# Projection, gate, up and down matmuls issued as four 32-column tiles inside a loop of 32-column tiles

## The chip, the cores and the metric

One core of one Trainium2 chip runs the whole kernel. The metric is device time in microseconds (us). The inputs are float32 (the feed-forward weights int32), the output is float32.

## What is computed

One transformer layer with adaptive layer norm over 2048 tokens of width 128 and 16 heads of width 8:

```python
h = _layernorm(x) * (1 + ca) + sa
x = x + ga * attention(h)      # 16 heads, softmax over 2048 keys, out @ Wo.T, clipped and projected
h = _layernorm(x) * (1 + cb) + sb
gate = h @ wg.T; up = h @ wu.T # wg, wu: 384 x 128, dequantised from int32
x = x + gb * ((silu(gate) * up) @ wd.T)
```

## The kernel before

The queries are cut into four blocks (`Bk`) of 512. A block is a loop of 64 steps: four groups of four heads, and for each group 16 tiles of 128 keys. In a step `j`

- `score` (line 686) multiplies 128 keys by 512 queries for four heads. The 128 keys are four **column tiles**: each matmul has 32 weight columns and writes 32 of the 128 output partitions, and `tile_position=(0, 32 * c)` says which quarter of TensorE's array it takes. Four matmuls in four quarters run at the same time. A step has 16 of them, bf16.
- ScalarE takes the exponential of the scores, 128x1024 at a time, twice in a step (line 506).
- `product(j - 1)` (line 702) multiplies the values by the exponentials of the step before. It is four float32 matmuls in four quarters, one for each head; the trace shows a float32 matmul as two weight loads and two matmul records, called passes in what follows, so a product has 8 records.

The closing work of block `Bk - 1` (output projection, residual, layer norm, feed-forward) is done while block `Bk` runs. Its place is written out by hand: TensorE issues its part behind `product` in fixed steps, `AT_WO` = 7 (output projection, line 711), `AT_TR` = 14 (transposes, line 718), `AT_GATE` = 18, 22, 27 (line 725), `AT_UP` = 20, 25, 30 (line 730) and `AT_DOWN` = 36, 38, 40, 42 (line 737). These matmuls have 128 weight columns and take the whole array. Gate and up are one matmul of 512 moving columns each (two passes). The output projection is four matmuls of 128 moving columns (8 passes), and a down step is three of them (6 passes). ScalarE takes a tanh (line 521) behind each gate, and it does so in the order written: in a gate step the tanh stands behind the step's two exponentials.

The last block's closing work has nothing to run beside it. It stands at the end: `t_wo`, seven and two filler matmuls (`keep_warm`, line 660) around the transposes, three gates and three ups in banks of their own, and 12 down matmuls (line 797).

TensorE's queue is in order. `score` of a step waits until ScalarE has emptied one of three PSUM slots, `product` waits for the exponentials of its own step.

Of the kernel before, what the change touches and what calls it, by code (L numbers as in the profile page):

```python
# [30 lines left out]
P = 128  # L31
# [10 lines left out]
CW = 32  # L42
COLS = P // CW
HID = 384
NM = HID // P
# [13 lines left out]
DOWN_BANK = (0, 3, 6, 7)  # L59
# [16 lines left out]
def build(nc, x, columns, wmod, fixed, w1t, w2t, w_att, wgt, wut, wdt, out):  # L76
    with ExitStack() as ctx:
        def sb(name, shape, dt=F32):
            return ctx.enter_context(nc.sbuf_tensor(name, shape, dt))

        def sem(name):
            return ctx.enter_context(nc.semaphore(name))
# [10 lines left out]
        wk_sb, wv_sb, wq_sb, wo_sb = (w_att_sb[:, i, :] for i in range(4))  # L93
# [16 lines left out]
        wg_f, wu_f = sb("wg_f", [P, HID]), sb("wu_f", [P, HID])  # L110
        wd_f = sb("wd_f", [P, NM, D])
# [13 lines left out]
        def tmp(words, *shape, dt=F32):  # L125
            v = arena[:, at[0]:at[0] + words]
            at[0] += words
            assert at[0] <= ARENA
            if dt != F32:
                v = v.bitcast(dt)  # L130
            if len(shape) == 2:
                v = v.rearrange("p (a b) -> p a b", a=shape[0])
            return v
# [32 lines left out]
        att_T = tmp(BT)  # L166
# [5 lines left out]
        h2_T = tmp(BT)  # L172
        th = [tmp(BT) for _ in range(NM)]
        gl = [tmp(BT) for _ in range(NM)]
        hid = tmp(NM * BT, NM, BT)
# [15 lines left out]
        def bank(i):  # L191
            return ps[:, i, :]
# [5 lines left out]
        O_bank, M_bank = bank(6), bank(7)  # L198
# [10 lines left out]
        S = {n: sem(n) for n in names}  # L209
# [332 lines left out]
        def _(pe):  # L542
# [3 lines left out]
            for i in range(2):  # L546
                ins = pe.matmul(bank(6 + i)[:, 0:3 * D], silu_b[:, :], wmod_sb[:, 3 * D * i:3 * D * (i + 1)],
                                start=True, stop=True)
# [108 lines left out]
            def keep_warm(n, to):  # L657

                for _ in range(n):
                    ins = pe.matmul(to, ones_bf[:, 0:P], ones_bf[:, 0:BT], start=True, stop=True)  # L660
                ins.then_inc(S["warm"], 1)
# [32 lines left out]
            def product(Bk, j):  # L694

                g, kt = divmod(j, NT)
                pe.wait_ge(S["exped"], Bk * 2 * STEPS + 2 * j + 2)
                if kt == 0 and not (isinstance(Bk, int) and Bk == 0 and g == 0):
                    pe.wait_ge(S["o_evac"], Bk * NG + g)
                for i in range(GH):  # L700
                    h = GH * g + i
                    ins = pe.matmul(O_bank[32 * i:32 * (i + 1), :], V_op[:, kt, VW * h:VW * h + 32],  # L702
                                    probs[:, 2 * (j % 2) + i // 2, BT * (i % 2):BT * (i % 2 + 1)],
                                    start=kt == 0, stop=kt == NT - 1, tile_position=(0, 32 * i))
                if kt == NT - 1:
                    ins.then_inc(S["pv_done"], 1)

            def t_wo(Bk):
                pe.wait_ge(S["norm"], Bk + 1)
                for t in range(TPB):  # L710
                    ins = pe.matmul(M_bank[:, P * t:P * (t + 1)], att_T[:, P * t:P * (t + 1)], wo_sb,  # L711
                                    start=True, stop=True)
                ins.then_inc(S["wo_ps"], 1)

            def t_transpose(Bk):
                pe.wait_ge(S["h2_done"], Bk + 1)
                for t in range(TPB):
                    ins = pe.transpose(M_bank[:, P * t:P * (t + 1)], h2[:, t, :], ident_sb)  # L718
                ins.then_inc(S["h2T_ps"], 1)

            def t_gate(Bk, m, to):
                pe.wait_ge(S["h2T_done"], Bk + 1)
                if m and to is M_bank:
                    pe.wait_ge(S["glu_done"], Bk * NM + m)
                pe.matmul(to, wg_f[:, P * m:P * (m + 1)], h2_T, start=True, stop=True).then_inc(S["gate_ps"], 1)  # L725

            def t_up(Bk, m, to):
                if to is M_bank:
                    pe.wait_ge(S["gated"], Bk * NM + m + 1)
                pe.matmul(to, wu_f[:, P * m:P * (m + 1)], h2_T, start=True, stop=True).then_inc(S["up_ps"], 1)  # L730

            def t_down(Bk, to, tiles=range(TPB)):
                if tiles[0] == 0:
                    pe.wait_ge(S["glu_done"], Bk * NM + NM)
                for t in tiles:
                    for m in range(NM):
                        ins = pe.matmul(to[:, P * t:P * (t + 1)], hid[:, m, P * t:P * (t + 1)], wd_f[:, m, :],  # L737
                                        start=m == 0, stop=m == NM - 1)
                if tiles[-1] == TPB - 1:
                    ins.then_inc(S["down_ps"], 1)  # L740

            def block_steps(Bk, tails, p):
                for j in range(STEPS):
                    score(Bk, j, p)
                    if j:
                        product(Bk, j - 1)
                    elif tails:
                        product(Bk - 1, STEPS - 1)
                    if tails:
                        if j == AT_WO:  # L750
                            t_wo(Bk - 1)
                        if j == AT_TR:
                            t_transpose(Bk - 1)
                        if j in AT_GATE:
                            t_gate(Bk - 1, AT_GATE.index(j), M_bank)
                        if j in AT_UP:
                            t_up(Bk - 1, AT_UP.index(j), M_bank)
                        if j in AT_DOWN:
                            t_down(Bk - 1, M_bank, [AT_DOWN.index(j)])

            def blocks(p):
                first, last = NB * p, NB * (p + 1) - 1
                if p == 0:
                    pe.wait_ge(S["K_ones"], 16)
                else:
                    pe.wait_ge(S["Q_loaded"], 16 * QUERY_LOADS * first)
                block_steps(first, False, p)
                if p == 0:
                    pe.wait_ge(S["ffn_ready"], 3)
                if p == 0:  # L770
                    for Bk in range(first + 1, last + 1):
                        pe.wait_ge(S["Q_loaded"], 16 * QUERY_LOADS * Bk)
                        block_steps(Bk, True, p)
                else:
                    with pe.Fori(first + 1, last + 1) as Bk:
                        pe.wait_ge(S["Q_loaded"], 16 * QUERY_LOADS * Bk)
                        block_steps(Bk, True, p)
                product(last, STEPS - 1)

                pe.wait_ge(S["o_evac"], NG * (last + 1))  # L780
                pe.matmul(bank(0)[96:128, :], place_num, O_sb[:, NG - 1, :], start=True, stop=True,
                          tile_position=(0, 96))
                pe.matmul(bank(1)[96:128, :], place_den, O_sb[:, NG - 1, :], start=True, stop=True,
                          tile_position=(0, 96)).then_inc(S["placed"], 1)
                t_wo(last)
                pe.wait_ge(S["epow_out"], 2 * (last + 1))
                keep_warm(7, bank(5))
                t_transpose(last)
                keep_warm(2, bank(5))
                for m in range(NM):  # L790
                    t_gate(last, m, bank(m))
                    t_up(last, m, bank(3 + m))

                for m in range(NM):
                    pe.wait_ge(S["glu_done"], last * NM + m + 1)
                    for t in range(TPB):
                        ins = pe.matmul(bank(DOWN_BANK[t])[:, P * t:P * (t + 1)], hid[:, m, P * t:P * (t + 1)], wd_f[:, m, :],
                                        start=m == 0, stop=m == NM - 1)
                ins.then_inc(S["down_ps"], 1)
                if p == 0:  # L800
                    pe.wait_ge(S["flag_in"], 1)
                    pe.matmul(bank(2)[0:1, 0:1], flag_f[:, 0:1], flag_f[:, 1:2], start=True, stop=True)\
                        .then_inc(S["flag_ps"], 1)
# [8 lines left out]
            with pe.If(pe.value_load(flag_i[0:1, 0:1], min_val=0, max_val=1)):  # L812

                q_all = q_slot(0)
                with pe.Fori(0, NB) as b:
                    pe.wait_ge(S["max_loaded"], 16 * PARTS * (b + 1))
                    for h in range(H):
                        for t in range(TPB):
                            pe.wait_ge(S["max_taken"], b * (H * TPB) + h * TPB + t + 1)
                            for i in range(NB):  # L820
                                ins = pe.matmul(bank(i), q_all(h, SHIFT_ROW)[:, P * t:P * (t + 1)],
                                                K_op[0:SHIFT_ROW, h, BT * i:BT * (i + 1)], start=True, stop=True)
                            ins.then_inc(S["max_scores"], 1)
                    pe.wait_ge(S["max_taken"], (b + 1) * (H * TPB) + 1)
                    for t in range(TPB):
                        ins = pe.transpose(M_bank[0:H, P * t:P * (t + 1)], mx[:, t, :], ident_sb)
# [434 lines left out]
```

## Time and profile before

| | us |
|---|---|
| median of 3 runs | 625.63 |
| lowest and highest | 624.21, 626.75 |
| the profiled execution: its time | 624.65 |
| its span, first to last instruction | 622.8 |
| TensorE busy | 565.1 |
| ScalarE busy | 526.5 |

The span is what the rows below divide up; 1.85 us lie outside it. Busy times of TensorE are of overlapping records, whose ends are modelled.

### The profile page before, as it was taken

To read this page: it belongs to the slowest core of one execution; us is meant where nothing else is said; L and a number is where in the kernel's file an instruction comes from. 1 tells how busy PE (TensorE), PEld (TensorE's weight loads), DVE (VectorE), ACT (ScalarE), POOL (GpSimd) and SP (SyncE) were. 2 spreads that over 40 slices of the span, in tenths; PEclk is the share of its full clock that TensorE was granted. 3 is DMA by queue.
4 is the path that set the end of the run, shared out by engine and by line. 5 is a ranking of instruction groups with operands and counts; after the bars stand their busy time and mean duration, and the time that the engine had idled before them with its cause. 6 is when DMAs were issued, how large, how long until landed. Compare 5 with 4: busy or idle time off the path is not lost.

```text
span 622.8 us, 14892 instructions
## 1 busy us (share of the span) xinstructions
PE 565.1 (91%) x6482; PEld 207.4 (33%) x6482; DVE 144.4 (23%) x403; ACT 526.5 (85%) x607; POOL 20.1 (3%) x23
## 2 busy tenths in 40 slices
PE   1688299999999999999999999999999999999635
PEld 0353033333333333333333333343333333433123
DVE  7957400000000531100004510000026110010264
ACT  3575499999999999899999989889999989899501
POOL 2300100000000000000000100000001000000010
PEclk9599599999999999999999999999999999999959
DMA  6014566610000400000004000000000000000000
GB/s 183 2 59 96 119 131 128 113 30 11 3 8 6 82 6 6 1 11 18 11 1 87 2 9 1 11 18 11 1 11 2 10 1 9 2 23 5 2 0 22
DMA packets 15617, 19.50 MB, mean 31 GB/s; under 512 B 2255, under 2 KB 13711, under 8 KB 15263
## 3 DMA queue, kind: packets, MB, share of 16 engines
q1 hardware_dynamic: 14927, 16.96, 12.8%
q0 software_dynamic: 336, 1.18, 0.6%
q8 instruction: 52, 0.85, 0.6%
q10 hardware_dynamic: 288, 0.40, 0.2%
q14 instruction: 14, 0.11, 0.1%
HBM read 12.10 MB, written 4.19 MB: 26 GB/s over the span
## 4 chain that ended last, share of the span: by engine, by line
PE 50%; ACT 33%; issue 8%; DVE 5%; DMA 3%; SPq 1%; POOL 0%; ACTq 0%
ACT probs L506 30%; PE ps L702 19%; PE ps L686 19%; DMA q_scr<-arena 2%; PE ps L725 2%; PE ps L730 2%; PE ps L737 2%; PE ps L660 1%; DVE probs L914 1%; PE ps L711 1%; DMA x_tm<-x_dram 1%; PE ps L597 1%; PE ps L603 1%; SPq L257 1%; PE ps L577 1%
## 5 line engine op out<-in xcount | busy, mean ns | idle before, releaser
L506 ACT ACTIVATE probs<-ps 128x1024 f32<-128x1024 f32 x512 | 473.9, 1084 | 21.4 <-PE ps L686 21.3
L702 PE MATMUL ps<-probs,V_op 128*32 128x512 f32 x2048 | 271.6, 602 | 1.7 <-ACT probs L506 1.1
L686 PE MATMUL ps<-Q_op,K_op 73*32 73x512 bf16 x4096 | 269.4, 379 | 1.0 <-ACT probs L506 1.0
L686 PEld LDWEIGHTS ps<-Q_op,K_op 73*32 73x32 bf16 x4096 | 114.7, 96 | 204.5 <-issue 135.2
L702 PEld LDWEIGHTS ps<-probs,V_op 128*32 128x32 f32 x2048 | 44.8, 108 | 94.2 <-ACT probs L506 85.8
L1055 DVE COPY O_sb<-ps 128x512 f32<-128x512 f32 x16 | 11.1, 691 | 254.5 <-PE ps L702 254.5
L357 POOL TENSOR_TENSOR small<-small,half 128x4 f32<-128x4 f32 x4 | 4.1, 1014 | 504.0 <-DVE small L1108 504.0
L1137 DVE SCALAR_TENSOR_TENSOR arena<-arena,ps 128x512 f32<-128x512 f32 x12 | 8.2, 687 | 43.6 <-ACT arena L521 43.6
L516 ACT ACTIVATE arena<-ps 128x512 f32<-128x512 f32 x4 | 2.4, 597 | 18.6 <-PE ps L718 18.6
L1143 DVE TENSOR_TENSOR arena<-ps,arena 128x512 f32<-128x512 f32 x12 | 8.3, 691 | 42.3 <-PE ps L730 42.2
L554 PE MATMUL ps<-fixed_sb,arena 128*128 128x128 f32 x32 | 6.8, 356 | 12.0 <-POOL arena L363 11.1
L1155 DVE TENSOR_TENSOR arena<-ps,mod 128x512 f32<-128x512 f32 x3 | 2.1, 692 | 63.4 <-PE ps L737 63.4
L660 PE MATMUL ps<-ones_bf 128*128 128x512 bf16 x16 | 7.2, 621 | 7.8 <-POOL small L357 7.8
L1078 DVE RECIPROCAL arena<-arena 128x512 f32<-128x512 f32 x4 | 13.4, 3354 | 0.1
L725 PE MATMUL ps<-arena,wg_f 128*128 128x512 f32 x24 | 13.3, 636 | 0.0
L730 PE MATMUL ps<-arena,wu_f 128*128 128x512 f32 x24 | 13.2, 632 | 0.0
L521 ACT ACTIVATE arena<-ps 128x512 f32<-128x512 f32 x12 | 7.2, 597 | 6.9 <-PE ps L725 6.9
L737 PEld LDWEIGHTS ps<-wd_f,arena 128*128 128x128 f32 x72 | 8.9, 190 | 10.1 <-issue 10.1
L620 PE MATMUL ps<-arena,hs_bf 128*16 128x512 bf16 x4 | 1.7, 434 | 10.9 <-ACT arena L452 10.9
L737 PE MATMUL ps<-wd_f,arena 128*128 128x128 f32 x72 | 11.2, 292 | 0.0
L451 ACT ACTIVATE arena<-arena 128x512 bf16<-128x512 f32 x4 | 2.5, 622 | 10.3 <-DMA q_scr<-arena 8.0
L711 PE MATMUL ps<-w_att_sb,arena 128*128 128x128 f32 x32 | 5.5, 326 | 5.7 <-DVE arena L1082 5.7
(150 smaller groups left out, 251.8 us busy)
## 6 DMA issues: line engine op xcount, KB each, us to landing
K_op<-k_scr SPq DMA_DIRECT2D x36, 128.0 KB
Q_op<-q_scr SPq DMA_DIRECT2D x9, 384.0 KB
arena<-O_sb SPq DMA_DIRECT2D x120, 16.0 KB
k_scr<-probs SPq DMA_DIRECT2D x9, 128.0 KB, 1.8
q_scr<-arena POOLq DMA_DIRECT2D x3, 384.0 KB, 15.0
Q_op<-q_scr SPq DMA_DIRECT2D x12, 96.0 KB
x_tm<-x_dram SPq DMA_DIRECT2D x4, 256.0 KB, 4.6
out_dram<-arena SPq DMA_DIRECT2D x4, 256.0 KB, 2.3
```

The costliest lines, as they stand in the source:

```text
L506: act.activation(probs[:, 2 * (j % 2) + half_, :], slot_bank(u % 3), ACT.Exp)\
L660: ins = pe.matmul(to, ones_bf[:, 0:P], ones_bf[:, 0:BT], start=True, stop=True)
L686: ins = pe.matmul(slot_bank(u % 3)[CW * c:CW * (c + 1), i, :], K_op[0:rows, h, at_k:at_k + CW], Q_op[0:rows, at_q:at_q + BT], start=True, ...
L702: ins = pe.matmul(O_bank[32 * i:32 * (i + 1), :], V_op[:, kt, VW * h:VW * h + 32], probs[:, 2 * (j % 2) + i // 2, BT * (i % 2):BT * (i % 2 ...
L711: ins = pe.matmul(M_bank[:, P * t:P * (t + 1)], att_T[:, P * t:P * (t + 1)], wo_sb, start=True, stop=True)
L725: pe.matmul(to, wg_f[:, P * m:P * (m + 1)], h2_T, start=True, stop=True).then_inc(S["gate_ps"], 1)
L730: pe.matmul(to, wu_f[:, P * m:P * (m + 1)], h2_T, start=True, stop=True).then_inc(S["up_ps"], 1)
L737: ins = pe.matmul(to[:, P * t:P * (t + 1)], hid[:, m, P * t:P * (t + 1)], wd_f[:, m, :], start=m == 0, stop=m == NM - 1)
L1055: dve.tensor_copy(O_sb[:, g, :], O_bank).then_inc(S["o_evac"], 1)
L1078: c.did(dve.reciprocal(rec_T, rec_T))
L1137: dve.scalar_tensor_tensor(gl[m], th[m], 1.0, gates, ALU.add, ALU.mult).then_inc(S["gated"], 1)
L1143: dve.tensor_tensor(hid[:, m, :], ups, gl[m], ALU.mult).then_inc(S["glu_done"], 1)
```

## The change

Each of these matmuls with 128 weight columns becomes four matmuls with 32, written to the four quarters of the same output. The moving operand, the data type, the places in the order and the waits stay as they are. The transposes and the filler matmuls are not touched.

```diff
+            def by_columns(to, weights, moving, start=True, stop=True):
+                for c in range(COLS):
+                    ins = pe.matmul(to[CW * c:CW * (c + 1), :], weights[:, CW * c:CW * (c + 1)], moving,
+                                    start=start, stop=stop, tile_position=(0, CW * c))
+                return ins
+
             def t_wo(Bk):
                 pe.wait_ge(S["norm"], Bk + 1)
                 for t in range(TPB):
-                    ins = pe.matmul(M_bank[:, P * t:P * (t + 1)], att_T[:, P * t:P * (t + 1)], wo_sb,
-                                    start=True, stop=True)
+                    ins = by_columns(M_bank[:, P * t:P * (t + 1)], att_T[:, P * t:P * (t + 1)], wo_sb)
                 ins.then_inc(S["wo_ps"], 1)
...
-                pe.matmul(to, wg_f[:, P * m:P * (m + 1)], h2_T, start=True, stop=True).then_inc(S["gate_ps"], 1)
+                by_columns(to, wg_f[:, P * m:P * (m + 1)], h2_T).then_inc(S["gate_ps"], 1)
...
-                pe.matmul(to, wu_f[:, P * m:P * (m + 1)], h2_T, start=True, stop=True).then_inc(S["up_ps"], 1)
+                by_columns(to, wu_f[:, P * m:P * (m + 1)], h2_T).then_inc(S["up_ps"], 1)
...
-                        ins = pe.matmul(to[:, P * t:P * (t + 1)], hid[:, m, P * t:P * (t + 1)], wd_f[:, m, :],
-                                        start=m == 0, stop=m == NM - 1)
+                        ins = by_columns(to[:, P * t:P * (t + 1)], hid[:, m, P * t:P * (t + 1)], wd_f[:, m, :],
+                                         start=m == 0, stop=m == NM - 1)
...
-                        ins = pe.matmul(bank(DOWN_BANK[t])[:, P * t:P * (t + 1)], hid[:, m, P * t:P * (t + 1)], wd_f[:, m, :],
-                                        start=m == 0, stop=m == NM - 1)
+                        ins = by_columns(bank(DOWN_BANK[t])[:, P * t:P * (t + 1)], hid[:, m, P * t:P * (t + 1)],
+                                         wd_f[:, m, :], start=m == 0, stop=m == NM - 1)
```

## Rows read from the trace of the kernel before

**Rows 1.** Busy time by stretch: first block, second block, the closing work at the end.
```profile
core 0: us, PE busy (x) PEld busy (x) DVE busy (x) ACT busy (x) POOL busy (x), PEclk, DMA share, GB/s
77.80:195.20 117.40, 116.65 (x1529) 40.22 (x1528) 2.74 (x8) 116.94 (x130) 0.00 (x0) 1.00 0.29 56
195.40:324.50 129.10, 128.72 (x1588) 45.85 (x1584) 22.67 (x52) 120.94 (x133) 2.05 (x2) 1.00 0.08 17
...
593.20:622.80 29.60, 14.99 (x59) 8.91 (x59) 15.84 (x50) 2.39 (x4) 2.01 (x2) 0.73 0.04 11
```

**Rows 2.** ScalarE by line in the second block: count, busy and mean, idle before, releaser.
```profile
L506 ACT ACTIVATE probs<-ps 128x1024 f32<-128x1024 f32 x129 | 120.0, 1071 | 7.0 <-PE ps L686 7.0
L521 ACT ACTIVATE arena<-ps 128x512 f32<-128x512 f32 x3 | 1.8, 597 | 1.2 <-PE ps L725 1.2
```

**Rows 3.** Timeline of ScalarE through the down steps: start, us, work, idle before.
```profile
268.73 3.78 ACT L506 ACTIVATE probs<-ps 128x1024 f32<-128x1024 f32 x4
273.26 3.77 ACT L506 ACTIVATE probs<-ps 128x1024 f32<-128x1024 f32 x4 [0.75 <-PE ps L686]
...
286.82 5.61 ACT L506 ACTIVATE probs<-ps 128x1024 f32<-128x1024 f32 x6 [0.75 <-PE ps L686]
```

**Rows 4.** Timeline of TensorE, a plain step.
```profile
207.78 1.06 PE L702 MATMUL ps<-probs,V_op 128*32 128x512 f32 x8
208.67 1.05 PE L686 MATMUL ps<-Q_op,K_op 73*32 73x512 bf16 x16
```

**Rows 5.** Timeline of TensorE around a down step and the step behind it.
```profile
270.73 1.07 PE L702 MATMUL ps<-probs,V_op 128*32 128x512 f32 x8
271.73 0.94 PE L737 MATMUL ps<-wd_f,arena 128*128 128x128 f32 x6
272.59 1.05 PE L686 MATMUL ps<-Q_op,K_op 73*32 73x512 bf16 x16
273.46 1.03 PE L702 MATMUL ps<-probs,V_op 128*32 128x512 f32 x8
274.32 1.04 PE L686 MATMUL ps<-Q_op,K_op 73*32 73x512 bf16 x16
```

**Rows 6.** Timeline around the output projection.
```profile
209.62 1.07 PE L702 MATMUL ps<-probs,V_op 128*32 128x512 f32 x8
210.61 1.16 PE L711 MATMUL ps<-w_att_sb,arena 128*128 128x128 f32 x8
211.70 1.05 PE L686 MATMUL ps<-Q_op,K_op 73*32 73x512 bf16 x16
212.37 1.02 ACT L506 ACTIVATE probs<-ps 128x1024 f32<-128x1024 f32 x1 [0.97 <-PE ps L686]
```

**Rows 7.** Timeline around the first gate (232.46) and the first up (237.17).
```profile
231.46 1.07 PE L702 MATMUL ps<-probs,V_op 128*32 128x512 f32 x8
232.46 1.12 PE L725 MATMUL ps<-arena,wg_f 128*128 128x512 f32 x2
233.52 1.05 PE L686 MATMUL ps<-Q_op,K_op 73*32 73x512 bf16 x16
233.62 0.60 ACT L521 ACTIVATE arena<-ps 128x512 f32<-128x512 f32 x1 [0.41 <-PE ps L725]
234.19 3.77 ACT L506 ACTIVATE probs<-ps 128x1024 f32<-128x1024 f32 x4
...
236.18 1.06 PE L702 MATMUL ps<-probs,V_op 128*32 128x512 f32 x8
...
237.17 1.13 PE L730 MATMUL ps<-arena,wu_f 128*128 128x512 f32 x2
238.23 1.05 PE L686 MATMUL ps<-Q_op,K_op 73*32 73x512 bf16 x16
...
238.90 1.94 ACT L506 ACTIVATE probs<-ps 128x1024 f32<-128x1024 f32 x2 [0.94 <-PE ps L686]
```

**Rows 8.** Gate and product by line: durations in ns, least, median, most.
```profile
L725 PE MATMUL ps<-arena,wg_f x24: 592/593/697, 232.5 to 611.8; 128*128 128x512 f32 x24
...
L702 PE MATMUL ps<-probs,V_op x2048: 589/593/617, 80.9 to 584.2; 128*32 128x512 f32 x187
```

**Rows 9.** Timeline of TensorE in the closing work at the end.
```profile
593.23 2.07 PE L711 MATMUL ps<-w_att_sb,arena 128*128 128x128 f32 x8 [5.74 <-DVE arena L1082]
...
607.84 1.13 PE L725 MATMUL ps<-arena,wg_f 128*128 128x512 f32 x2
608.80 1.02 PE L730 MATMUL ps<-arena,wu_f 128*128 128x512 f32 x2
...
612.24 1.02 PE L730 MATMUL ps<-arena,wu_f 128*128 128x512 f32 x2
613.10 2.84 PE L797 MATMUL ps<-wd_f,arena 128*128 128x128 f32 x24
```

**Rows 10.** Records begun in a tenth of a microsecond, at a product (columns as in the first group).
```profile
229.70:229.80 0.10, 0.06 (x4) 0.09 (x8) 0.00 (x0) 0.10 (x1) 0.00 (x0) 1.00 0.00 0
```

## The prediction

> **What bounds the kernel now.** I read the busy time by stretch first. The first block, which carries no closing work, takes 117.4 us for 64 steps, 1.83 us each, and ScalarE is busy for 116.94 of them; the second block takes 129.1 us, and ScalarE is busy for 120.94 [rows 1]. So the exponentials set the pace of a plain step: two of them at 0.92 us. TensorE has little to spare, though. Scores and product without a wait between them take 0.87 + 0.86 = 1.73 us (273.46 less 272.59, and 274.32 less 273.46) [rows 5], which leaves 0.10 us a step. Anything put into TensorE's order beyond that starves ScalarE.
>
> Next, ScalarE by line in the second block, to see how it waits. It stood idle for 7.0 us before exponentials, always for scores, and for 1.2 us before the three tanh, for the gate matmuls [rows 2]. The timeline says where: 0.97 us behind the output projection [rows 6], 0.94 behind an up, 0.41 before a tanh [rows 7], 0.75 behind each of four down steps [rows 3]. 0.97 + 3 x 0.94 + 4 x 0.75 is 6.8 of the 7.0. These 8 us are what the change can take from a block; the other 3.5 of the 11.7 that block two has over block one are mainly the copy and the tanh themselves, which stay.
>
> **What a closing matmul costs in TensorE's order.** I measure it from the start of the product before it to the start of the scores behind it, less the 0.89 us that this takes in a plain step [rows 4].
> - down: 272.59 - 270.73 - 0.89 = 0.97 us [rows 5]
> - output projection: 211.70 - 209.62 - 0.89 = 1.19 [rows 6]
> - gate: 233.52 - 231.46 - 0.89 = 1.17; up: 238.23 - 236.18 - 0.89 = 1.16 [rows 7]
>
> A gate is two passes of 512 columns. One pass takes 0.43 us: eight of them lie between 608.80 and 612.24 [rows 9]. Two are 0.86, so 0.31 us of the 1.17 are not streaming. Part of it is seen in the durations: the first gate pass has 697 ns where most have 593, 0.10 more, a weight load that nothing hides; a product behind a wait has 617, 0.02 more [rows 8], for a quarter of the columns. The remaining 0.2 is silence on either side, where full-width and quarter-width matmuls meet. Where quarter meets quarter there is none: product to scores takes 0.86 [rows 5], float32 followed by bf16, just two passes.
>
> A short pass, 128 moving columns at full width, takes (2.84 - 0.275)/23 = 0.112 us in the last 24, with 0.275 the duration of one record, worked out from the modelled end [rows 9].
>
> **The change part by part.** In the new form a gate or up is what `product` already is: eight records in four quarters, 0.86 us, with the weights of the next pass loaded under the present one [rows 5]. That takes the gate from 1.17 to 0.86 and the up from 1.16 to 0.86.
>
> A short pass in quarters is not in the trace. From below it can't beat a quarter of a long one, 0.43/4 = 0.107. From above, the densest sustained stream there is is the scores, four pairs of weight load and matmul in 0.87/4 = 0.217 us [rows 5]. I take 0.11: right after an event wait eight loads and four matmuls begin inside 0.10 us [rows 10], so four pairs in 0.11 us ask for little more than TensorE does here, and 32 weight columns expose 0.02 us where 128 expose 0.10 [rows 8], so the loads fit under a pass. The output projection is then 8 x 0.11 = 0.88 instead of 1.19, a down step 6 x 0.11 = 0.66 instead of 0.97. Each of the eleven insertions of a block gets 0.30 to 0.31 us shorter.
>
> **What of it reaches ScalarE.** For the eight without a tanh, idle time is insertion less 0.22: 0.97 for 1.19, 0.94 for 1.16, 0.75 for 0.97. The same 0.22 each time means that TensorE alone sets these waits, and that the next steps don't make them good. The new insertions stay above 0.22, so the whole saving arrives: 0.31 + 3 x 0.30 + 4 x 0.31 = 2.45 us a block.
>
> In a gate step the tanh stands between. It starts when the gate is done, 2.16 us after the product's start (233.62 - 231.46) [rows 7]. New: 0.89 for the product, 0.43 to the second pass, 0.59 for that record, 0.04 for the semaphore, 1.95. The tanh comes 0.21 earlier, and the exponential behind it 0.57 after the tanh, at 1.95 + 0.57 = 2.52. The scores would let it start at 0.89 + 0.86 + 0.67 = 2.42 (0.67 is scores to exponential, 238.90 - 238.23 [rows 7]), so the tanh decides: 3 x 0.21 = 0.63 us a block.
>
> A block saves 2.45 + 0.63 = 3.1 us, three blocks 9.3. The first block has no closing work and stays.
>
> At the end everything is on the path. The output projection runs at the low clock (mean 0.73 in this stretch [rows 1]), its 8 passes are streaming, and only the first load shrinks: 0.1. The first gate pass has 593 + 104 ns there too, gain 0.08; the five projections behind it follow without gaps and stay; 24 down passes gain 24 x 0.002 = 0.05 [rows 9]. Sum 0.2.
>
> All in all 9.5 us. From the profiled execution's 624.65 that is 615.2; the median of the runs lies 1.0 above that execution, so 625.63 - 9.5 = 616.1 us. What the edit costs is instructions: 3 more pairs for each of the old, 528 pairs in all. What hides them is the streaming of the passes themselves, 0.11 us for four pairs; without that cover the third rival below holds.
>
> **A rule and the rows.** Why the 0.2 us of silence vanishes is no row's to tell: no full-width matmul behind quarter-width ones comes without it. The Trainium skill ("TensorEngine Tiling (Array Packing)", Key Properties) says that changing the tiling mode, and not merely the tile, drains TensorE. By that rule the silence goes with the change, and the sum is the 9.5 us. Were it a matter of the closing work itself, only the weight load would shrink, and the sum would be the second rival's.
>
> **Rivals.**
> 1. *The sum holds* (0.68): 616.1, with its own range 614.8 to 618. The lower end is passes of 0.107 (0.3 us) and the scatter of a median of few runs, the upper one gates and ups that give 0.2.
> 2. *The silence stays*: only the weight loads shrink, 0.10 to 0.02, 0.08 us x 33 insertions + 0.2 = 2.8 us, 622.8. Against it: quarter after quarter has no silence at any of the places shown. 0.07.
> 3. *The short passes are bound by issue*, the case on the other side. Four pairs must be issued where one was, and a short pass gives them 0.11 us. There are 32 short passes in each of three blocks and 24 at full clock at the end, 120. The gain of 9.5 is used up when a pass takes 0.11 + 9.5/120 = 0.19 us; above that the kernel is slower. At 0.217, the pace of the scores, it is 120 x 0.107 = 12.8 lost, 3.3 net: 628.9. At the pace of a whole step, 24 pairs in 1.73, a pass takes 0.29, and it is 638. For it: nothing in the trace issues faster for longer than a dozen instructions. Against it: those dozen, at 0.008 us each [rows 10]. 0.10. The Trainium skill ("TensorE: Matmul & The Clock Gate", the section on the gap of 56 ns) has two floors that bear on it, about 25 ns from matmul to matmul, which four in 0.11 us just meet, and about 62 ns a matmul where ucode decodes, which would make a pass 0.25. This trace's four matmuls inside 0.1 us speak against the second.
> 4. *The short passes are a little long*: four loads of 0.02 to 0.03 us one behind the other instead of together make a pass some 0.135. 120 x 0.025 = 3 us given back: 619.1, range 618 to 621.5. 0.12.
>
> The remaining 0.03 is for what I don't see, half of it a wait that the earlier output projection meets.
>
> **How the numbers follow.** A measurement of this kernel tells about 0.5%, 3.1 us, from no change; faster is below 622.5, slower above 628.8. Case 1 and 4 are faster, 0.80, and with the rest 0.81. Case 2 lies on the border and counts as same, with a part of the others, 0.09. Slower is case 3, 0.10. The likeliest time is 616.1. The range reaches from 614.5 over cases 1 and 4 to 621.5 and leaves out 2, 3 and the rest, 0.2.
>
> **What the new profile would show.** The second block's stretch goes from 129.1 to 126.0. ScalarE's idle time: 0.66 behind the output projection, 0.64 behind an up, 0.44 behind a down step, 0.20 before a tanh. Product to scores over a gate 1.75 (was 2.06), over a down step 1.55 (was 1.86). The first quarter-width gate record begins 0.87 to 0.89 after the product's and has at most 620 ns. Down records of one quarter begin 0.11 apart; 0.2 or more would be the third rival, 1.0 from product to gate the second. The transposes keep their silence. The prediction is wrong if a short pass takes over 0.15, or if the product's own records get longer where closing matmuls follow.

## The result and the profile after

The changed kernel takes 615.55 us (median of 4 runs, 614.81 to 616.19) against 625.59 before; the ratio is 0.984, with a 95% interval of 0.9815 to 0.9865. The forecast was 616.1. Its profiled execution has a span of 613.0 us where that of before had 622.8.

The stretches of the second block and of the closing work at the end, in the windows view:

```profile
core 0: us, PE busy (x) PEld busy (x) DVE busy (x) ACT busy (x) POOL busy (x), PEclk, DMA share, GB/s
77.80:195.20 117.40, 116.98 (x1529) 40.38 (x1528) 2.69 (x7) 116.82 (x129) 0.00 (x0) 0.99 0.28 57
195.40:321.40 126.00, 125.62 (x1724) 47.63 (x1724) 22.68 (x52) 120.98 (x134) 2.05 (x2) 1.00 0.09 18
...
583.00:613.00 30.00, 14.61 (x190) 7.57 (x191) 16.01 (x51) 2.39 (x4) 2.02 (x2) 0.67 0.04 12
```

The windows are cut by eye. From the first exponential of a block to the first of the next, worked out from the start times in the trace, the second block took 129.12 us before and takes 125.76 now; the first takes 117.33 in both. The third and fourth block save the same. Three blocks with closing work save 3.36 us each, 10.1 in all, and in this profiled execution the end saves nothing.

TensorE around the first gate and the first up, and around a down step, which answer to [rows 7] and [rows 5]. All the changed matmuls are recorded under the helper's line 710 and told apart by their tiles:

```profile
231.20 1.07 PE L702 MATMUL ps<-probs,V_op 128*32 128x512 f32 x8
232.06 1.07 PE L710 MATMUL ps<-arena,wg_f 128*32 128x512 f32 x8
232.91 1.07 PE L686 MATMUL ps<-Q_op,K_op 73*32 73x512 bf16 x16
...
235.66 1.07 PE L702 MATMUL ps<-probs,V_op 128*32 128x512 f32 x8
236.55 1.04 PE L710 MATMUL ps<-arena,wu_f 128*32 128x512 f32 x8
237.40 1.05 PE L686 MATMUL ps<-Q_op,K_op 73*32 73x512 bf16 x16
...
272.97 1.07 PE L702 MATMUL ps<-probs,V_op 128*32 128x512 f32 x8
273.85 0.84 PE L710 MATMUL ps<-wd_f,arena 128*32 128x128 f32 x24
274.51 1.05 PE L686 MATMUL ps<-Q_op,K_op 73*32 73x512 bf16 x16
```

The first gate begins 0.86 us after the product (it was 1.00) and the scores 0.85 after the gate (1.06). The ups and the other two gates begin 0.88 after their product, which had itself to wait for an exponential, as in a plain step. A gate or up is now just streaming. The transposes, which were left at full width, still begin 1.00 us after the product, before (223.53 to 224.53) and now (223.27 to 224.26). Over a down step it is 274.51 - 272.97 = 1.54 us from product to scores, where it was 1.86.

ScalarE's timeline through a block, which answers to [rows 3, 6, 7]:

```profile
212.11 12.94 ACT L506 ACTIVATE probs<-ps 128x1024 f32<-128x1024 f32 x14 [0.63 <-PE ps L686]
...
233.18 0.60 ACT L521 ACTIVATE arena<-ps 128x512 f32<-128x512 f32 x1 [0.23 <-PE ps L710]
233.68 3.77 ACT L506 ACTIVATE probs<-ps 128x1024 f32<-128x1024 f32 x4
238.06 3.77 ACT L506 ACTIVATE probs<-ps 128x1024 f32<-128x1024 f32 x4 [0.62 <-PE ps L686]
...
270.98 3.77 ACT L506 ACTIVATE probs<-ps 128x1024 f32<-128x1024 f32 x4 [0.41 <-PE ps L686]
275.17 3.77 ACT L506 ACTIVATE probs<-ps 128x1024 f32<-128x1024 f32 x4 [0.42 <-PE ps L686]
```

Idle time is 0.63 behind the output projection (0.66 was forecast), 0.62 behind an up (0.64), 0.42 behind a down step (0.44), 0.21 to 0.23 before a tanh (0.20). Four exponentials and a down step take 275.17 - 270.98 = 4.19 us; before it was (286.82 - 273.26)/3 = 4.52 [rows 3].

### The profile page after: what moved, and what is told of

It reads as the page before. It is cut to its first block, busy times and chain, and to the rows that moved or that the text cites. A ratio compares the mean times of both kernels' runs of the same rounds, so it can differ in the third digit from the quotient of the medians.

```text
span 613.0 us, 15946 instructions
## 1 busy us (share of the span) xinstructions
PE 553.6 (90%) x7008; PEld 211.1 (34%) x7010; DVE 144.4 (24%) x403; ACT 525.9 (86%) x607; POOL 20.1 (3%) x23
## 3 DMA queue, kind: packets, MB, share of 16 engines
HBM read 12.10 MB, written 4.19 MB: 27 GB/s over the span
## 4 chain that ended last, share of the span: by engine, by line
PE 49%; ACT 33%; issue 8%; DVE 5%; DMA 3%; SPq 1%; POOL 0%; ACTq 0%
ACT probs L506 31%; PE ps L702 20%; PE ps L686 19%; PE ps L710 6%; DMA q_scr<-arena 2%; DVE probs L919 1%; PE ps L660 1%; DMA x_tm<-x_dram 1%; PE ps L597 1%; PE ps L603 1%; PE ps L577 1%; DVE arena L1083 1%; ACT arena L417 1%; PE ps L547 0%; SPq L257 0%
## 5 line engine op out<-in xcount | busy, mean ns | idle before, releaser
L686 PEld LDWEIGHTS ps<-Q_op,K_op 73*32 73x32 bf16 x4096 | 120.8, 96 | 197.7 <-issue 145.9
L1148 DVE TENSOR_TENSOR arena<-ps,arena 128x512 f32<-128x512 f32 x12 | 8.3, 692 | 40.1 <-PE ps L710 40.0
L710 PEld LDWEIGHTS ps<-wd_f,arena 128*32 128x32 f32 x384 | 11.0, 110 | 7.8 <-issue 7.8
L710 PE MATMUL ps<-arena,wg_f 128*32 128x512 f32 x96 | 12.9, 605 | 0.0
L710 PE MATMUL ps<-wd_f,arena 128*32 128x128 f32 x384 | 12.9, 273 | 0.0
L710 PE MATMUL ps<-arena,wu_f 128*32 128x512 f32 x96 | 12.5, 592 | 0.0
L554 PEld LDWEIGHTS ps<-fixed_sb,arena 128*128 128x128 f32 x32 | 4.6, 179 | 17.1 <-issue 8.4
```

What stands on the lines that cost most here:

```text
L554: ins = pe.transpose(bank(b % 2)[:, P * t:P * (t + 1)], src[:, TPB * b + t, :], ident_sb)
L686: ins = pe.matmul(slot_bank(u % 3)[CW * c:CW * (c + 1), i, :], K_op[0:rows, h, at_k:at_k + CW], Q_op[0:rows, at_q:at_q + BT], start=True, ...
L710: ins = pe.matmul(to[CW * c:CW * (c + 1), :], weights[:, CW * c:CW * (c + 1)], moving, start=start, stop=stop, tile_position=(0, CW * c))
L1148: dve.tensor_tensor(hid[:, m, :], ups, gl[m], ALU.mult).then_inc(S["glu_done"], 1)
```

## The experiments

Whole times are beside the kernel before, timed on the same chip: 624.9 us for the first four kernels, 626.2 for the next four, 625.8 for the last two. Such a time carries a start of its own: from kernel to kernel the first exponential begins between 78.5 and 82.3 us into the profiled execution, in code that none of the edits touches. So each is also judged by its second block, first exponential to first exponential. A block's time comes from one profiled execution; the third block agrees with the second to 0.01 us where the table gives no other number.

| kernel | time, us | ratio to before, interval | second block, us |
|---|---|---|---|
| before | 625.59 | | 129.12 |
| changed | 615.55 | 0.984 (0.9815 to 0.9865) | 125.76 |
| quarters for the short passes only | 620.37 | 0.9927 (0.989 to 0.9963) | 127.91, the third 127.45 |
| quarters for gate and up only | 620.45 | 0.9925 (0.99 to 0.995) | 127.42 |
| halves instead of quarters | 623.02 | 0.9966 (0.9944 to 0.9988) | 128.53 |
| full width, down in 12 pieces | 629.98 | 1.0077 (1.0053 to 1.0102) | 130.60 |
| quarters, down in 12 pieces | 613.25 | 0.9815 (0.9768 to 0.9862) | 124.73 |
| quarters, everything in pieces | 611.41 | 0.9769 (0.9729 to 0.981) | 123.98 |
| quarters, the end at full width | 617.47, one run | | 126.32, the third 125.77 |
| quarters, down with 64 moving columns | 615.36, one run | | 125.83 |
| quarters, down in 24 pieces | 610.55 | 0.9763 (0.9734 to 0.9792) | 123.94 |
| quarters, everything in small pieces | 608.79 | 0.973 (0.9701 to 0.9759) | 123.17 |

### One part of the change at a time

```diff
 # first kernel: gate and up as before
-                by_columns(to, wg_f[:, P * m:P * (m + 1)], h2_T).then_inc(S["gate_ps"], 1)
+                pe.matmul(to, wg_f[:, P * m:P * (m + 1)], h2_T, start=True, stop=True).then_inc(S["gate_ps"], 1)
...
 # second kernel: output projection and down as before
-                        ins = by_columns(to[:, P * t:P * (t + 1)], hid[:, m, P * t:P * (t + 1)], wd_f[:, m, :],
+                        ins = pe.matmul(to[:, P * t:P * (t + 1)], hid[:, m, P * t:P * (t + 1)], wd_f[:, m, :],
...
```

> Only the short passes (output projection, down) are in quarters; gate and up stay at full width. Theory A, that a silence of about 0.2 us plus a bare weight load stands at each place where full width meets quarter width and goes insertion by insertion: ScalarE idles 0.63 us behind the output projection and 0.42 behind a down step, and still 0.94 behind an up and 0.41 before a tanh; 0.31 + 4 x 0.33 = 1.6 us a block, 4.9 in all, about 620.7 us. Rival B, that the short passes lose by issuing four times as many and that the gates and ups carry the whole gain: 624 or more.

> Only gate and up are in quarters; output projection and down stay at full width. Theory A: idle time 0.62 behind an up, 0.21 before a tanh, 0.97 and 0.75 at the others as before; 3 x (0.32 + 0.20) = 1.6 us a block, 4.7 in all, about 620.9 us. With the first run the two parts add up to the whole, 9.6 to 10. Rival B: nearly the whole gain, 616 to 617 us.

The times are 620.37 and 620.45 us, and the idle times are those of theory A to 0.03 us, but for the output projection in the first kernel's second block. The parts add up: the third block of the first kernel saves 1.67 us and a block of the second 1.70, together 3.37 where the whole change has 3.36. By whole times it is 4.5 and 4.5 us, 9.0 where 9.6 to 10 were expected, which is within their scatter. The first kernel's second block is 0.46 longer than its third, and the timeline of that block shows why:

```profile
212.35 1.07 PE L702 MATMUL ps<-probs,V_op 128*32 128x512 f32 x8
...
212.93 0.69 DVE L1087 TENSOR_TENSOR arena<-arena 128x512 f32<-128x512 f32 x1
...
213.68 1.08 PE L710 MATMUL ps<-w_att_sb,arena 128*32 128x128 f32 x32 [0.26 <-DVE arena L1087]
...
215.23 1.02 ACT L506 ACTIVATE probs<-ps 128x1024 f32<-128x1024 f32 x1 [1.10 <-PE ps L686]
```

The normalised attention (line 1087) was done 0.06 us before the output projection that reads it, and TensorE, in order, waited with everything behind it. In the changed kernel's own trace the same instruction ends about half a microsecond ahead of the projection (210.02 against 210.58). The kernel with its end at full width met the same in its second block (126.32 against 125.77 in its third). This placement has little margin; the prediction had kept half of its last 0.03 for such a wait.

### Halves: is it the width or the change of width?

```diff
-                for c in range(COLS):
-                    ins = pe.matmul(to[CW * c:CW * (c + 1), :], weights[:, CW * c:CW * (c + 1)], moving,
-                                    start=start, stop=stop, tile_position=(0, CW * c))
+                for c in range(2):
+                    ins = pe.matmul(to[64 * c:64 * (c + 1), :], weights[:, 64 * c:64 * (c + 1)], moving,
+                                    start=start, stop=stop, tile_position=(0, 64 * c))
```

> All the changed matmuls are issued as two tiles of 64 columns instead of four of 32, each in its half of the array, between loop matmuls that stay in quarters. Theory A, a change of tile width makes TensorE run dry: the silence stays as at full width and only the bare weight load shrinks, 0.10 to 0.05: product to scores over a gate 2.00 us, over a down step 1.81, idle 0.89 behind an up, about 624 us. Rival C, only the full-width form runs dry and any tiles flow into each other: product to scores 1.75 and 1.55, 616 us. Rival D, the silence goes with the width of the weights: half the gain, 620.5 us.

Theory A holds; 623.02 us where it had about 624. TensorE around the first gate:

```profile
231.00 1.07 PE L702 MATMUL ps<-probs,V_op 128*32 128x512 f32 x8
232.01 1.08 PE L710 MATMUL ps<-arena,wg_f 128*64 128x512 f32 x4
233.01 1.05 PE L686 MATMUL ps<-Q_op,K_op 73*32 73x512 bf16 x16
```

Halves are tiles too, they run side by side, and they still begin 1.00 us after the product, like the full width. Product to scores is 2.01 us (2.00 expected); the same over a down step is 1.80 (1.81 expected), and ScalarE idles for 0.89 us behind an up, as expected. Only the first load got shorter: a matmul of 512 columns has at most 697 ns at full width [rows 8], 593 for the ups in quarters, and 643 here (by line; least, median and most in ns):

```profile
L710 PE MATMUL ps<-arena,wu_f x48: 592/592/643, 236.7 to 610.9; 128*64 128x512 f32 x48
```

So the silence belongs to the meeting of two tile widths, quarters with halves or with the full array, and not to full width. That is what the Trainium skill ("TensorEngine Tiling (Array Packing)", Key Properties) states: a new tiling mode drains TensorE, a new tile of the same mode doesn't. This trace agrees, and gives the size: 1.17 - 0.86 = 0.31 us for the way there and back at full width, of which 0.10 is the bare load [rows 7, 8]. Rivals C (616 us) and D (620.5) are out. Whether the new width waits for the whole engine or only for the tiles that it overlaps, no run here can tell: a half or the full array overlaps quarters in every one of them.

### The same pieces at full width and in quarters

Both kernels cut the four down steps of six passes into twelve of two, at every second step; the result on VectorE and its store move behind the third evacuation (that move was not tried by itself; the prices below are read at the pieces).

```diff
-AT_DOWN = (36, 38, 40, 42)
+AT_DOWN = tuple(range(34, 58, 2))
...
-                            t_down(Bk - 1, M_bank, [AT_DOWN.index(j)])
+                            t_down_piece(Bk - 1, AT_DOWN.index(j))   # one (t, m) of the twelve
```

> The kernel before, at full width, with the four down steps of six passes cut into twelve of two passes, at every second step from 34 to 56; the result is taken after the third evacuation instead of before it. The matmuls are the same. Theory A, the silence is paid at each insertion: 2 x 0.112 + 0.31 = 0.53 us each, idle 0.53 - 0.22 = 0.31 behind each of twelve, 3.7 us a block where it was 3.0, about 627.8 us. Rival E, the extra time belongs to the amount of closing work and not to the insertion: the pieces of 0.25 us would lie within the slack of 0.2 us that two steps have, 3 us a block are won, about 617 us.

> The changed kernel (quarters) with the down steps cut into the same twelve pieces at the same steps as in the run before. Theory A: without a silence a piece costs two passes, 0.22 us, and two steps have 0.20 us of slack (3.67 for the four exponentials against 3.46 for TensorE): ScalarE no longer idles behind the down pieces or by under 0.05, where four steps cost 0.52 each (4.19 between them, less 3.67); 1.6 to 2.1 us a block, 609.5 to 611 us. Rival F, that every piece has a fixed price in quarters too (a first load, a semaphore): 0.1 or more each, 1.2 us a block, no gain over 613 us.

The same cut makes one kernel slower and the other faster: by the second block 1.48 us longer than before at full width, and 1.03 shorter than the changed kernel in quarters. The whole times, 629.98 and 613.25 us, show the first; the second is too scattered (611.32 to 616.04) to be told from the changed kernel's 615.55 by them alone. At full width each piece leaves ScalarE idle for 0.30 us, and there are twelve; in quarters the view shows no idle time at all, 68 exponentials in one run:

```profile
272.63 3.77 ACT L506 ACTIVATE probs<-ps 128x1024 f32<-128x1024 f32 x4 [0.33 <-PE ps L686]
276.70 3.77 ACT L506 ACTIVATE probs<-ps 128x1024 f32<-128x1024 f32 x4 [0.30 <-PE ps L686]
```

```profile
259.50 63.48 ACT L506 ACTIVATE probs<-ps 128x1024 f32<-128x1024 f32 x68 [0.62 <-PE ps L686]
```

Both sums were off, though. At full width a block lost 1.5 us, not 0.7. In quarters it won 1.0, not 1.6 to 2.1, which is nearer to rival F's 1.2 and its 613 us than to theory A. Two steps with four exponentials take 117.33/32 = 3.67 us when nothing is in the way; what an insertion costs, its price, is the distance beyond that. Its length is, as in the prediction, product to scores less the 0.89 us of a plain step:

| insertion | its length, us | two steps, us | its price, us |
|---|---|---|---|
| down, six passes, full width [rows 3, 5] | 0.97 | 4.52 | 0.85 |
| down, six passes, quarters | 1.54 - 0.89 = 0.65 | 4.19 | 0.52 |
| down, two passes, full width | 276.03 - 274.62 - 0.89 = 0.52 | 276.70 - 272.63 = 4.07 | 0.40 |
| down, two passes, quarters | 270.04 - 268.94 - 0.89 = 0.21 | 272.69 - 268.94 = 3.75 | 0.08 |

The last two rows come from these timelines of TensorE, at full width and in quarters:

```profile
274.62 1.06 PE L702 MATMUL ps<-probs,V_op 128*32 128x512 f32 x8
275.61 0.49 PE L746 MATMUL ps<-wd_f,arena 128*128 128x128 f32 x2
276.03 1.05 PE L686 MATMUL ps<-Q_op,K_op 73*32 73x512 bf16 x16
```

```profile
268.94 1.06 PE L702 MATMUL ps<-probs,V_op 128*32 128x512 f32 x8
269.82 0.40 PE L710 MATMUL ps<-wd_f,arena 128*32 128x128 f32 x8
270.04 1.05 PE L686 MATMUL ps<-Q_op,K_op 73*32 73x512 bf16 x16
...
272.69 1.06 PE L702 MATMUL ps<-probs,V_op 128*32 128x512 f32 x8
```

The price is the length less 0.12 or 0.13 in all four. It is 0.10 more than the idle time because exponentials back to back overlap by 0.10 (1.02 us long, 0.92 apart), and an idle gap loses that too. And the spare time of the second step doesn't help: TensorE spends it before its product, waiting for the exponential that the product reads, and can't run ahead. That was my mistake in both sums: at full width I counted idle time only, in quarters I set the piece against the slack of two steps. Whether the 0.08 of the last row is a rest of the length or rival F's fixed price for every piece, this table alone can't say; smaller pieces can, below.

### Everything in pieces

```diff
+AT_WO, AT_TR, AT_GATE = (7, 8), 15, (18, 27, 36)     # the other half of a gate one step earlier
+AT_UP = (20, 21, 23, 24), (29, 30, 32, 33), (38, 39, 41, 42)
+AT_DOWN = (44, 46, 47, 49, 51, 52, 54, 56, 57, 59, 61, 62)
```

> All closing work in quarters and in pieces: output projection two tiles at steps 7 and 8, each gate as two halves of 256 columns in neighbouring steps, each up as four pieces of 128, down as twelve. The matmuls are the same in sum. Theory A: a block comes close to TensorE's own work, 64 x 1.73 + 0.88 + 6 x 0.86 + 12 x 0.22 + 0.70 for the transposes = 120.1 us; with stalls where pieces stand in neighbouring steps 121.5 to 123, where the changed kernel has 125.8: 604 to 608 us. Rival F: pieces have a price of their own, 614 us or more.

A miss: 611.41 us, 3.4 over the range, and 123.98 for a block, 1.0 over; rival F's 614 is missed too, from below. TensorE's work is a bound, but not one that can be neared by spreading pieces of 0.22 us, each of which costs 0.08 or more wherever it stands.

### The end, and short passes half as short

```diff
 # first kernel: behind the last block, full width
+            def at_full(to, weights, moving, start=True, stop=True):
+                return pe.matmul(to, weights, moving, start=start, stop=stop)
...
 # second kernel: down steps in the loop
+                    for n in range(2):
+                        for m in range(NM):
+                            ins = by_columns(to[:, P * t + 64 * n:P * t + 64 * (n + 1)], hid[:, m, P * t:P * (t + 1)],
+                                             wd_f[:, m, 64 * n:64 * (n + 1)], start=m == 0, stop=m == NM - 1)
```

> The changed kernel with the closing work at the end, behind the last block, at full width again; that inside the loop stays in quarters. The prediction's terms for the end: 0.1 us for the first load of the output projection and 0.08 for the first gate come back, 0.2 us in all from the last exponential to the end, if the clock rises at the same place. Rival: the end is not changed by the form, and what differs there is the moment at which the clock rises.

> The changed kernel with its down steps in the loop as 12 passes of 64 moving columns instead of 6 of 128: the same streaming, twice the instructions, 96 begun where 48 were. A pass of 64 columns streams in 0.055 us. If issue is nowhere near binding: passes 0.055 to 0.06 apart, product to scores 1.54 to 1.60 us, idle 0.42 to 0.48. If four matmuls can't be begun in under 0.1 us (the third rival's mechanism, with its threshold between 0.055 and 0.109): passes 0.1 apart, product to scores 2.1, idle about 1.0.

From the start of the last exponential to the end it is 40.30 us before, 40.49 in the changed kernel and 40.19 with the end at full width again. What differs most is the clock: before, the granted clock rose from 0.50 to 1.00, from 1.2 to 2.4 GHz, 0.3 us before the first gate; in the changed kernel it rose 0.6 us after the gate's start (a mean of 0.50 from 597 to 598 and 0.78 from 598 to 599), and a gate record lasts up to 902 ns where 593 is usual. Ahead of it both had the same filler matmuls and transposes.

The gates of the changed kernel by line:

```profile
L710 PE MATMUL ps<-arena,wg_f x96: 591/592/902, 232.1 to 602.0; 128*32 128x512 f32 x96
```

Where the clock is up in time, the smaller first load does show. The first gate and the first up of the end, in the changed kernel and in the one with down in 12 pieces, whose end is written the same:

```profile
597.83 1.34 PE L710 MATMUL ps<-arena,wg_f 128*32 128x512 f32 x8
599.00 1.03 PE L710 MATMUL ps<-arena,wu_f 128*32 128x512 f32 x8
...
594.68 1.06 PE L710 MATMUL ps<-arena,wg_f 128*32 128x512 f32 x8 [0.26 <-ACT arena L516]
595.57 1.04 PE L710 MATMUL ps<-arena,wu_f 128*32 128x512 f32 x8
```

From this gate to its up it is 0.96 us at full width (607.84 to 608.80 [rows 9], and the same in the two other kernels with full-width gates and an early clock), 0.88 or 0.89 in all six kernels with quarter-width gates and an early clock, and 1.17 in the changed kernel. The clock rose behind the first gate's start in three of the twelve profiled executions: the changed kernel's, the halves' and that of the kernel with quarters for the short passes only, whose gates are at full width. So the late rise does not go with the form. With an early clock, the whole stretch is 40.2 to 40.4 us in the three kernels whose end is at full width and 39.4 to 40.1 in the five whose end is in quarters. That agrees with a gain of 0.2, but five single executions of differing kernels don't prove its size.

The second kernel settles the third rival. Twelve passes of 64 columns, 48 matmuls and as many loads, take 0.66 us:

```profile
270.50 0.85 PE L710 MATMUL ps<-wd_f,arena 128*32 128x64 f32 x48
271.16 1.05 PE L686 MATMUL ps<-Q_op,K_op 73*32 73x512 bf16 x16
```

Product to scores is 1.55 us and the idle time 0.43, as expected if issue does not bind. By the start times a pass is 0.056 us after the one before. That is 0.007 us for each instruction of its four pairs, against 0.027 at the pace of the scores.

### A rule for small pieces

If the price is length less 0.13, a piece of 0.11 us is free. The smallest that the kernel can cut is one float32 matmul with 64 moving columns.

```diff
-AT_DOWN = (36, 38, 40, 42)
+AT_DOWN = tuple(range(34, 58))                      # one of 24 pieces in every step
...
 # last kernel, all closing work
+AT_GATE = (17, 18, 19), (27, 28, 29), (37, 38, 39)  # 128, 128, 256 columns
+AT_UP = tuple(range(21, 27)), tuple(range(31, 37)), tuple(range(41, 47))   # 4 x 64, 2 x 128
+AT_DOWN = tuple(range(48, 63))                      # 24 pieces in 15 steps
```

> The changed kernel with its down steps cut into 24 pieces of one float32 matmul with 64 moving columns in quarters (0.11 us each), one in every step from 34 to 57. Theory G, formed from the runs so far: an insertion of length I costs I - 0.13 us whatever the distance to the next, because TensorE's spare tenth lies before each product, in a wait for an exponential, and can't be saved up (prices 0.85 for 0.98, 0.52 for 0.655, 0.40 for 0.53, 0.084 for 0.218). Pieces of 0.11 are then free, in every step: a block goes from 125.76 to 123.7 us, no stretch of exponentials from step 34 on longer than 0.92 us each, about 609.3 us. Rival H, slack is a matter of the average: 0.11 a step is over the 0.10 that TensorE has, and one in each step costs as much as 0.22 in every second, a block 124.7, 612.5 us. Rival I, each piece has a price: more than that.

> The version with all closing work in pieces, from the same rule: gates as 128, 128 and 256 columns in neighbouring steps, ups as four pieces of 64 and two of 128 in six steps, down as 24 pieces of 64 in fifteen steps, nine of them with two. Theory G: gates 2 x 0.09, ups 2 x 0.09, down 9 x 0.09 a block, 1.9 us, and 0.6 for the output projection in two halves, as in the run before; 1.2 us a block under the 123.98 of the version with larger pieces, 122.8, about 607.5 us. Rival H: neighbouring pieces add up and a block stays at 124, 611 us.

The first of the two takes 610.55 us (609.3 by theory G) and 123.94 for a block (123.7). Down is nearly free: 68 exponentials from the last up on take 62.67 us, 0.8 less than with pieces of 0.21, and the four down steps' 2.08 us a block have shrunk by 1.82. The rest is about 0.25 us over 24 steps. A part of it is TensorE's bound: its step is now 0.87 + 0.86 + 0.11 = 1.84 us where the exponentials want 1.83 (1.8375 and 1.8333 by the start times, 0.1 over 24 steps), and it goes from piece to piece without a wait:

```profile
270.95 1.08 PE L686 MATMUL ps<-Q_op,K_op 73*32 73x512 bf16 x16
271.82 1.07 PE L702 MATMUL ps<-probs,V_op 128*32 128x512 f32 x8
272.68 0.32 PE L710 MATMUL ps<-wd_f,arena 128*32 128x64 f32 x8
272.79 1.08 PE L686 MATMUL ps<-Q_op,K_op 73*32 73x512 bf16 x16
```

The other part stands where the next group of heads begins:

```profile
293.00 1.07 PE L686 MATMUL ps<-Q_op,K_op 73*32 73x512 bf16 x16
293.16 0.69 DVE L1072 COPY O_sb<-ps 128x512 f32<-128x512 f32 x1 [28.72 <-PE ps L702]
293.99 1.06 PE L702 MATMUL ps<-probs,V_op 128*32 128x512 f32 x8
```

The group's first product waits until VectorE has copied out the sums of the group before, 0.99 us after the scores instead of 0.87. The same stop is in the first block of the kernel before (1.05 us between two exponentials there, where 0.92 is usual), and that kernel makes it good in the steps behind, at 3.61 us for four exponentials instead of 3.67. Here, with a piece in every step, TensorE can't, and 0.12 us stay.

So a piece of 0.11 us has hardly a price even in every step: theory G's 123.7 is 0.24 off and rival H's 124.7 is 0.76 off. A fixed price of 0.08 for each of 24 pieces would have been 1.9 us, so rivals F and I are out.

The last kernel, 608.79 us (607.5 by theory G), is the fastest of all by its median and by its block, 2.7% under the kernel before. Its block of 123.17 missed the 122.8 by 0.4. Two of its steps in a row with a piece of 0.22 us:

```profile
246.55 1.04 PE L709 MATMUL ps<-probs,V_op 128*32 128x512 f32 x8
247.41 0.40 PE L717 MATMUL ps<-arena,wu_f 128*32 128x128 f32 x8
247.63 1.05 PE L693 MATMUL ps<-Q_op,K_op 73*32 73x512 bf16 x16
248.50 1.04 PE L709 MATMUL ps<-probs,V_op 128*32 128x512 f32 x8
```

Such a step takes 248.50 - 246.55 = 1.95 us, 0.11 over the 1.83 of a plain one, where the rule had 0.09. The product no longer waits: it starts 0.87 us behind the scores, and full steps in a row leave TensorE no spare tenth to take off. A block has 21 pieces of this length, and 21 x 0.02 would be the 0.4; that the stops where a group begins have a part in it is not ruled out. So the rule of length less 0.13 holds for a piece with an easier step before it, and not "whatever the distance to the next", as theory G had it.

## Why the prediction was right

The forecast was 616.1, the time is 615.55, and the mechanism is the one of the first case. That the two lie only 0.5 us apart is in part luck: the blocks saved 0.8 us more than forecast and the end, in the profiled execution, 0.4 less. Point by point:

- **The silence and the bare load go.** Forecast 0.86 for both. By the prediction's own measure (product to scores less 0.89) the up went from 1.16 to 0.85 and the gates from 1.17 and 1.16 to 0.85; only the first is at 232.91 - 231.20 - 0.89 = 0.82, because the product before it had not waited and the 0.89 takes off 0.03 too much. That the silence comes from the change of tile width was argued there and in no row of before; the halves showed it.
- **A short pass takes 0.11 us.** 0.109 by the start times; in the loop a down step is 0.65 us long (0.66 forecast). The third rival, issue, is far off: the threshold was 0.19 a pass, and passes of 0.056 run without a gap. Four matmuls in 0.056 us are 14 ns each, which is below both floors that the prediction weighed under this rival; neither binds when the four go to four quarters. The second rival predicted 1.0 from product to gate, the trace has 0.86. The fourth, loads one after the other, would have made passes of 0.135.
- **Idle time is insertion less 0.22.** Right as a difference, which is all that the sum used, and it held within 0.01 (0.63 for 0.87, 0.62 for 0.85, 0.42 for 0.65). As a price it is wrong by the lost overlap of 0.10, which stayed hidden while the number of insertions stayed the same, and came out when the pieces changed it. Eight such losses, 0.8 us, are also in the 3.5 us a block that the prediction put down mainly to the copy and the tanh.
- **A block saves 3.1 us.** It saved 3.36. Output projection 0.34 (0.97 - 0.63) for 0.31, ups 0.32 each for 0.30, down 0.33 for 0.31, and the three gate steps 3.36 - 0.34 - 0.96 - 1.32 = 0.74 for 0.63: the exponential now follows the tanh after 0.50 us (233.68 - 233.18), not 0.57. Here the prediction misread its rows. The 0.57 was no distance that the tanh sets: before, the exponential started 234.19 - 233.52 = 0.67 us after the scores, as behind an up, so it was the scores that it had waited for. Now it starts 0.77 after them, and it is the tanh that decides, as forecast, but at 233.68 - 231.20 = 2.48 us after the product and not 2.52. Small shortfalls in one direction, 0.8 us in all.
- **The end saves 0.2 us.** In the profiled execution it took 0.2 us more than before. The output projection got 0.13 shorter (2.07 to 1.94 us), and the first gate, at the low clock for its first 0.6 us, lost 0.21 (0.96 to 1.17). The term of 0.08 for the gate's first load is right where the clock is up in time: 0.96 to 0.88 in six other kernels.

## What to carry to other kernels

Work inserted into a loop of tiled matmuls should take the loop's tile width, even where the full array would do: every change of width cost 0.3 us there and back, on an engine that had 0.1 to spare. Once the change of width is gone, the way to hide such work is to cut it to the spare time of a single step, one piece to a step; slack that an engine spends waiting for its partner can't be saved up for a larger piece later. It isn't useless either: the kernel before used it to make good a stop behind it, and steps filled to the brim can't. The price of a stall is read from the distance between iterations, not from the idle column, which leaves out the overlap that the stall breaks.

## What the runs showed that I had not expected

TensorE began 48 float32 matmuls and 48 weight loads of 32 columns in 0.66 us, 7 ns for each, without a gap in the streaming: four matmuls of 64 moving columns, side by side in the four quarters, every 0.056 us. Two tiles of 64 columns run dry against four of 32 just as the undivided array does (1.00 us from product to gate in both). And bf16 behind float32, or the reverse, costs nothing that shows when the tile width stays: 0.85 us from gate to scores and 0.86 from product to scores, 0.87 from scores to product where the product need not wait (272.59 to 273.46 [rows 5]).
